# Mixture-of-experts kernel: chunks routed one by one, POOL left with indirect DMAs alone, one region per expert, tiles in two rounds of 24 and 47

## The reference

```python
x = x + relu(conv3x3_8_groups(ln_c(x)) + bias)
t = to_tokens(x)                                   # 4096 tokens of 128
flat = ln_t(t)
logits = flat @ router_w.T                         # 8 experts
topk_vals, topk_idx = top_k(logits, 2)
topk_w = softmax(topk_vals)
y_e = (silu(flat @ w_gate[e]) * (flat @ w_up[e])) @ w_down[e]   # 128 -> 256 -> 128
t = t + sum over a token's two experts of topk_w * y_e
```

## Time and profile before

| | |
|---|---|
| three runs, median (lowest to highest) | 278.57 us (277.93 to 279.11) |
| span of the profiled execution | 277.2 us |
| its own time | not given beside the span; the median lies 1.4 us over the span |
| TensorE busy (matmuls) | 202.9 us, 73% |
| POOL busy | 163.6 us, 59% |
| DVE busy | 140.8 us, 51% |
| ACT busy | 119.0 us, 43% |
| mean granted TensorE clock | 0.866 |

### The profile page before, as it was taken

The page is one execution under the profiler, slowest core; times in us unless marked ns, Lnnn a source line. Parts: engine busy times, 40 slices in busy tenths (PEclk is TensorE's granted clock), DMA queues, the critical chain, the costliest instruction groups (busy, mean ns, idle before and its releaser), DMA issues.

```text
span 277.2 us, 4518 instructions
## 1 busy us (share of the span) xinstructions
PE 202.9 (73%) x1186; PEld 174.3 (63%) x1186; DVE 140.8 (51%) x457; ACT 119.0 (43%) x285; POOL 163.6 (59%) x184
## 2 busy tenths in 40 slices
PE   6699576975529595739998654993999999999000
PEld 5687464864428484428887544883898789898000
DVE  3557696555241724445755322451458866555025
ACT  2369544745902353073453322342445454454100
POOL 5644388743775277725777777764356576666600
PEclk9599895999957777757999999898899999999855
DMA  7993010100133351100232232343239523361075
GB/s 235 380 381 116 0 48 30 53 29 10 48 94 82 78 115 59 48 10 31 74 87 70 68 78 78 100 134 84 61 68 303 159 72 96 99 195 43 15 237 217
DMA packets 26648, 28.99 MB, mean 105 GB/s; under 512 B 4957, under 2 KB 18409, under 8 KB 26624
## 3 DMA queue, kind: packets, MB, share of 16 engines
q1 hardware_dynamic: 21776, 20.03, 25.1%
q0 software_dynamic: 4544, 8.47, 9.1%
q10 hardware_dynamic: 304, 0.20, 0.2%
HBM read 16.93 MB, written 12.67 MB: 107 GB/s over the span
## 4 chain that ended last, share of the span: by engine, by line
PE 28%; POOL 21%; issue 13%; DVE 12%; DMA 11%; SPq 6%; ACT 6%; POOLq 1%; ACTq 0%; DVEq 0%
POOL zs L992 11%; POOL yb L1005 9%; PE ps_gu L349 7%; PE ps_y L439 5%; DMA yb<-y,zt 3%; PE ps_gu L419 3%; PE ps_gu L421 3%; PE ps_gu L420 3%; PE ps_h L429 3%; SPq L303 3%; DMA zt<-zs 3%; ACT zr L547 2%; DMA spare<-yb 2%; PE ps_z L408 2%; DVE bn L637 2%
## 5 line engine op out<-in xcount | busy, mean ns | idle before, releaser
L1005 POOL DMA_INDIRECT yb<-y,zt x78 | 76.3, 978 | 40.0 <-ACT y L583 24.6
L992 POOL DMA_INDIRECT zs<-zr,slot x64 | 63.0, 984 | 38.0 <-issue 18.3
L349 PE MATMUL ps_gu<-pad,ckw 128*128 128x256 f32 x192 | 53.7, 439 | 0.0
L349 PEld LDWEIGHTS ps_gu<-pad,ckw 128*128 128x128 f32 x192 | 41.7, 224 | 7.1
L842 DVE TENSOR_TENSOR hh<-ps_gu,sg 128x512 f32<-128x512 f32 (+1 forms) x40 | 27.1, 678 | 35.7 <-ACT sg L574 35.7
L439 PE MATMUL ps_y<-wall,hT 128*128 x312 | 41.9, 278 | 0.0
L439 PEld LDWEIGHTS ps_y<-wall,hT 128*128 128x128 f32 x312 | 38.7, 195 | 0.1
L574 ACT ACTIVATE sg<-ps_gu 128x512 f32<-128x512 f32 (+1 forms) x40 | 23.5, 586 | 33.3 <-PE ps_gu L421 33.3
L583 ACT ACTIVATE y<-ps_y,zt 128x128 f32<-128x128 f32 x78 | 24.4, 365 | 30.1 <-PE ps_y L439 30.1
L419 PE MATMUL ps_gu<-wall,z_lo 128*128 x78 | 36.4, 467 | 0.0
L408 PE MATMUL ps_z<-ident,zt 128*128 128x128 f32 x78 | 17.1, 302 | 21.2 <-DMA zt<-zs 15.2
(11 more groups left out here) (131 smaller groups left out, 225.9 us busy)
## 6 DMA issues: line engine op xcount, KB each, us to landing
zt<-zs SPq DMA_DIRECT2D x78, 65.0 KB, 2.0
spare<-yb SPq DMA_DIRECT2D x16, 256.0 KB, 4.5
xt<-x_rows SPq DMA_DIRECT2D x8, 256.0 KB, 5.3
xc<-x_cols SPq DMA_DIRECT2D x8, 256.0 KB, 6.6
spare<-gate_up_w SPq DMA_DIRECT2D x8, 256.0 KB, 6.3
out<-xt SPq DMA_DIRECT2D x8, 256.0 KB, 3.0
yb<-y,zt POOLq DMA_INDIRECT x78, 2.3
zs<-nulls SPq DMA_DIRECT2D x18, 65.0 KB, 3.3
```

What stands on the lines that cost most here:

```text
L349: last = nc.tensor.matmul(dst, ckw[:, h * BANDS + k, :], pad[n % 2][:, h * IMG:(h + 1) * IMG, below:below + PAIRS, dx:dx + WW], start=k == ...
L992: nc.gpsimd.indirect_dma_start(zs[g], bass.IndirectOffsetOnAxis(slot[:, k, n * TT + t:n * TT + t + 1], 0), zr[n % ZR][:, t, k, :], None, b ...
L1005: nc.gpsimd.indirect_dma_start(yb, bass.IndirectOffsetOnAxis(zt[:, u % RING, s, P:P + 1].bitcast(U32), 0), y[u % YB][:, s, :], None, bound ...
```

## The change

The order of routing changes from batches of chunks to single chunks, and what POOL does is cut down to constants, three weight tails and indirect DMAs.

- The power -0.5 of both LayerNorms goes from POOL to a square root on ACT (deviation_x, deviation_t) and five small operations on DVE (inverse_x, inverse_t: a reciprocal, one Newton step and the shift).
- rows_and_logits is one product with the identity and the router weights side by side (136 columns); ACT copies the logits and the rows out.
- top_two takes for each tile a max of 8 and a max_index of 8, then two compares with expert numbers. It runs for each chunk in the iteration after its convolution; slots, inverse_t and normalise_t of chunk n-2 run in iteration n. Those of the last chunk's LayerNorm run ahead of unit 0.
- zr has a buffer for each of the 8 chunks, with the token numbers written by POOL at the start. A row has 129 values: the weight no longer travels with it. The weights (gaps, shares, write_shares) are taken once for all tokens in units 3 to 7 and applied by DVE in add_rows, eight operations of 128 columns for a chunk. y_rows becomes one copy.
- POOL scatters all chunks first (dispatch), and only then results.
- There is one region per expert for all tokens. Round 1 has the first 24 full tiles of chunks 0 to 3 (first_table), round 2 the 47 others, sorted by the chunk that completes them (second_table): 12 + 24 = 36 units.
- RING goes from 8 to 18 and the y buffers from 8 to 16 (in the memory of the raw weights).
- SP gathers and stores by chunk: chunks 0 to 3 ahead of unit 30's load, then each later chunk as soon as the last unit that can hold its rows is stored.

The core of the diff:

```diff
-BATCHES = [(0, 1), (1, 2), (2, 4), (4, 6), (6, 8)]
-SETS = [(0, 3), (3, 5)]
-LAST = len(BATCHES) - 1
-SET_OF_BATCH = [g for g, (b0, b1) in enumerate(SETS) for _ in range(b0, b1)]
-BATCH_OF = [b for b, (c0, c1) in enumerate(BATCHES) for _ in range(c0, c1)]
-SET_CHUNKS = [(BATCHES[b0][0], BATCHES[b1 - 1][1]) for b0, b1 in SETS]
-BT = 2 * TT
-NT = [(c1 - c0) * TT for c0, c1 in SET_CHUNKS]
-GOFF = [c0 * N for c0, c1 in SET_CHUNKS]
-CAP = [nt * P + P for nt in NT]
-TILES = [2 * nt + E - 1 for nt in NT]
-SLOTS = [(t + 1) // 2 for t in TILES]
-FIRST = [sum(SLOTS[:g]) for g in range(len(SETS))]
+EARLY = CHUNKS // 2
+CAP = TOK + P
+NULL = E * CAP
+TILES1 = EARLY * N * 2 // P - E
+TILES2 = (CHUNKS - EARLY) * N * 2 // P + 2 * E - 1
+ROUNDS = [TILES1, TILES2]
+SLOTS = [(t + 1) // 2 for t in ROUNDS]
+FIRST = [0, SLOTS[0]]
 UNITS = sum(SLOTS)
-SET_OF_UNIT = [g for g, s in enumerate(SLOTS) for _ in range(s)]
-COUNT = [min(2, TILES[g] - 2 * (u - FIRST[g])) for u, g in enumerate(SET_OF_UNIT)]
-
+ROUND_OF_UNIT = [r for r, s in enumerate(SLOTS) for _ in range(s)]
+COUNT = [min(2, ROUNDS[r] - 2 * (u - FIRST[r])) for u, r in enumerate(ROUND_OF_UNIT)]
+LATE = CHUNKS - EARLY + 1
+NG = LATE * E
+
+
+def last_unit_of(n):
+    tiles = (max(n, EARLY - 1) + 1) * N * 2 // P + E - 1
+    return FIRST[1] + (tiles - TILES1 + 1) // 2 - 1
+
+
+X_GROUPS = [(0, 1), (1, 2), (2, 4), (4, 6), (6, 8)]
+DVE_TAILS = {2: [1, 3], 3: [5, 6], 4: [7]}
 POOL_TAILS = [0, 2, 4]
-DVE_TAILS = [[1, 3], [5, 6], [7]]
-X_GROUPS = [(0, 1), (1, 2), (2, 4), (4, 6), (6, 8)]
-
-ROW = P + 2
+
+ROW = P + 1
 WROW = 2 * 2 * H + 2 * P
-RING = 8
-YB = 8
-ZR = 4
+FUSED = P + E
+RING = 18
+YB = 16
 NOWHERE = 1 << 20
-PIECE = 4
-TABLE_UNIT = 10
+GATHER_AFTER = 30
+TABLE_UNIT = 8
 
 
 def metaformer_moe(nc, x_rows, x_cols, conv_k, conv_b, router, gate_up_w, down_w, out):
...
+            sp.wait_ge(table_ready, 1)
+            for n in range(EARLY):
+                sp.wait_ge(scattered[n], 16 * 2 * TT)
+            for u in range(0, FIRST[1], 4):
+                load_units(u, min(u + 4, FIRST[1]))
+            pad_regions()
+            for n in range(EARLY, CHUNKS):
+                sp.wait_ge(scattered[n], 16 * 2 * TT)
+            sp.wait_ge(nulls_stored, 16 * (E + 1))
+            sp.wait_ge(table_ready, 2)
+            for u in range(FIRST[1], GATHER_AFTER, 4):
+                load_units(u, min(u + 4, GATHER_AFTER))
+            await_results(EARLY - 1)
+            for n in range(EARLY):
+                gather_rows(n)
+            for u in range(GATHER_AFTER, UNITS, 4):
+                load_units(u, min(u + 4, UNITS))
+            await_results(EARLY)
+            gather_rows(EARLY)
+            for n in range(EARLY):
+                store_rows(n)
+            for n in range(EARLY + 1, CHUNKS):
+                await_results(n)
+                gather_rows(n)
+                store_rows(n - 1)
+            store_rows(CHUNKS - 1)
+            sp.wait_ge(out_stored, 16 * CHUNKS)
 
...
             def rows_and_logits(n):
-                b = BATCH_OF[n]
                 pe.wait_ge(t_ready, n + 1)
-                if n >= 2:
-                    pe.wait_ge(t_copied, n - 1)
+                if n >= 1:
+                    pe.wait_ge(t_copied, n)
                 for t in range(TT):
-                    last = nc.tensor.transpose(ps_t[n % 2][:, t * P:(t + 1) * P], xc[:, n, t * P:(t + 1) * P], ident[:])
+                    last = nc.tensor.matmul(ps_t[:, t // 2, t % 2, :], xc[:, n, t * P:(t + 1) * P], ident_x[:],
+                                            start=True, stop=True)
                 last.then_inc(t_rows_ready, 1)
...
+                nc.scalar.copy(logits[:, n * TT:(n + 1) * TT, :].rearrange("p (b t) e -> p b t e", b=2),
+                               ps_t[:, :, :, P:FUSED]).then_inc(logits_ready, 1)
+                nc.scalar.copy(xt[:, n * TT:(n + 1) * TT, :].rearrange("p (b t) c -> p b t c", b=2),
+                               ps_t[:, :, :, 0:P]).then_inc(t_copied, 1)
+
+            def deviation_t(n):
+                i = slice(n * TT, (n + 1) * TT)
+                act.wait_ge(mv2_ready, n + 1)
+                nc.scalar.activation(sd2[:, i], mv2[:, i, 1], ACT.Sqrt, bias=eps[:, 1:2]).then_inc(sd2_ready, 1)
 
             def normalise_t(n):
-                b = BATCH_OF[n]
-                act.wait_ge(rstd2_ready, b + 1)
+                act.wait_ge(rstd2_ready, n + 1)
                 act.wait_ge(t_copied, n + 1)
-                if n >= ZR:
-                    act.wait_ge(scattered[n - ZR], 16 * 2 * TT)
                 for t in range(TT):
                     i = n * TT + t
-                    last = nc.scalar.activation(zr[n % ZR][:, t, :, 0:P], xt[:, i:i + 1, :].broadcast_to([P, 2, P]),
-                                                ACT.Identity, bias=nmr2[:, i:i + 1], scale=rstd2[:, i:i + 1])
-                last.then_inc(z_ready, 1)
...
+            deviation_x(0)
             normalise_x(0)
+            deviation_x(1)
             act.wait_ge(pads_zeroed, 2)
             pad_evens(0)
...
+            for n in range(1, CHUNKS + 1):
+                conv_relu(n - 1, 1)
+                if n == 1:
+                    normalise_x(2)
+                if n in (2, 4):
+                    deviation_x(n // 2 + 2)
+                if n >= 3:
+                    deviation_t(n - 2)
+                    normalise_t(n - 2)
                 if n < CHUNKS:
                     conv_relu(n, 0)
+                copy_rows(n - 1)
                 if n + 1 < CHUNKS:
                     pad_evens(n + 1)
-                if n >= 1:
-                    copy_rows(n - 1)
-                if n < 2:
-                    for e in range(4 * n, 4 * n + 4):
-                        weight_heads(e)
-                for b, (c0, c1) in enumerate(BATCHES[:-1]):
-                    if n == c1:
-                        pair_weight(b)
-                        normalise_t(c0)
-                    if n == c1 + 1 and c1 == c0 + 2:
-                        normalise_t(c0 + 1)
+                if n == 1:
+                    deviation_t(0)
+                    normalise_t(0)
+                if n + 2 < CHUNKS:
+                    normalise_x(n + 2)
+                if 2 <= n <= 6:
+                    weight_heads((1, 3, 5, 6, 7)[n - 2])
+            deviation_t(CHUNKS - 1)
+            normalise_t(CHUNKS - 1)
             z_heads(0)
             for u in range(UNITS + 2):
                 if u + 1 < UNITS:
                     z_heads(u + 1)
                 if u < UNITS:
                     silu(u)
-                if u == 0:
-                    pair_weight(LAST)
-                if u <= 1:
-                    normalise_t(CHUNKS - 2 + u)
+                if u == 4:
+                    shares()
...
-                    last = nc.scalar.activation(y[u % YB][:, s, :], ps_y[u % 2][:, s * P:(s + 1) * P], ACT.Identity,
-                                                scale=zt[:, u % RING, s, P + 1:P + 2])
-                last.then_inc(y_ready, 1)
...
+            def inverse_t(n):
+                i = slice(n * TT, (n + 1) * TT)
+                dve.wait_ge(sd2_ready, n + 1)
+                nc.vector.reciprocal(guess2[:, i], sd2[:, i]).then_inc(dev2_step, 1)
+                dve.wait_ge(dev2_step, 4 * n + 1)
+                nc.vector.scalar_tensor_tensor(off2[:, i], mv2[:, i, 1], EPS_FFN, guess2[:, i], ALU.add, ALU.mult
+                                               ).then_inc(dev2_step, 1)
+                dve.wait_ge(dev2_step, 4 * n + 2)
+                nc.vector.scalar_tensor_tensor(half2[:, i], off2[:, i], -0.5, guess2[:, i], ALU.mult, ALU.mult
+                                               ).then_inc(dev2_step, 1)
+                dve.wait_ge(dev2_step, 4 * n + 3)
+                nc.vector.scalar_tensor_tensor(rstd2[:, i], half2[:, i], 1.5, guess2[:, i], ALU.add, ALU.mult
+                                               ).then_inc(dev2_step, 1)
+                dve.wait_ge(dev2_step, 4 * n + 4)
                 nc.vector.scalar_tensor_tensor(nmr2[:, i], mv2[:, i, 0], -1.0, rstd2[:, i], ALU.mult, ALU.mult
                                                ).then_inc(rstd2_ready, 1)
 
...
+            def top_two(n):
+                dve.wait_ge(logits_ready, n + 1)
+                for t in range(TT):
+                    last = nc.vector.max(top8[:, n * TT + t, :], logits[:, n * TT + t, :])
+                last.then_inc(top_ready, 1)
+                dve.wait_ge(top_ready, n + 1)
+                for t in range(TT):
+                    last = nc.vector.max_index(which8[:, t, :], top8[:, n * TT + t, :],
+                                               logits[:, n * TT + t, :])
+                last.then_inc(which_ready, 1)
+                dve.wait_ge(which_ready, n + 1)
+                for k in range(2):
+                    last = nc.vector.tensor_tensor(oh[:, k], ioe[:, k],
```

(65 more changed lines are left out.)

790 lines of the change are left out of this document (334 added, 456 removed).

## The result

The changed kernel takes 247.87 us (median of four runs, 246.16 to 248.83), the kernel before 278.25 us beside it (four runs, 277.71 to 279.11): a ratio of 0.891, 95% interval 0.887 to 0.896. Ratios here leave out executions more than 1.5% above the fastest of the same kernel; medians take all. The forecast was 245. The profiled execution has a span of 245.9 us and a time of its own of 248.08.

The account below looks back on a forecast made before the run. TensorE was held by 23 us of gaps from late scatters and a ring of 8, then by 2.94 us units. 109.7 + 5 + 35 x 2.94 = 217.6; + 9.3 + 16.8 = 243.7; + 1.4 = 245.1, range 234 to 258.

Parts of the forecast that it names:

- a ring of 8 and POOL's alternating scatters: Between routing and full expert work: tile loads wait for combines and late scatters; the 23 us of TensorE gaps go.
- POOL was to catch up at unit 12: Combines start at 128, 2.55 us a unit against results 2.94 apart, so POOL catches up at unit 12.
- Tiles: Expert stage: 36 units instead of 40, 4 x 2.94 = 11.8 us less, exact while TensorE is the limit.
- Routing: Routing stage: a DVE and ACT loop of 10.5 us sets the chunks; first gate-up at 109.7, no gain at its end.
- R1: First residual in routing, forecast at 21.2 us, against 22.14 before.
- R2 to R3: Second to third residual in routing, forecast as 7.9 us, putting R3 at 41.5.
- The searches: top_two in the routing loop: eight searches at 0.16 us each plus 0.6, 1.9 us per chunk.
- The rival of two passes: Index search in routing loads its values first: 5 to 7 us more, 250 to 252; chance 0.23.
- The table load: Silu's table load on ACT in round 1: 1.28 us by the trace, 2.66 by the skill, giving 245 or 246.5.
- Half clock in routing: Rival: TensorE at half clock through routing, 13.6 us a chunk instead of 10.5, +19, 264; chance 0.09.
- Round 1: First 12 units, 109.7 to about 150: 5 us added to the pace (3 to 10) for second table and slow first unit.
- The tail: After last gate-up: 9.3 us to the end of sum 3, sums 1.8 each, then 16.8 of gather, sum, store turns.

Follow-up runs that it names:

- kernel 4: The kernel before, with all of the last two chunks scattered by POOL before its first combine, rings still 8 units: 278.0 us beside 277.4, ratio 1.002.
- kernel 5: The kernel before, with rings of 16 units for tiles and results in place of 8: 271.0 us, ratio 0.980.
- kernel 6: The kernel before, with both rings of 16 units and all scatters ahead of the first combine: 270.3 us, ratio 0.977.
- kernel 12: The kernel before, with rings of 16, all scatters first, and the first set's gather and sums 4 and 8 units later: 263.4 us, ratio 0.949.
- kernels 1 and 8: Kernel 1: the changed kernel, with the last two chunks' scatters put between the combines of units 0 to 7, 263.4 us; for the other see kernel 8.
- kernel 7: The changed kernel, with every max and max_index of the routing stage done a second time into unread buffers: 252.8 us.
- kernel 10: The changed kernel, with VectorE's second table split over units 2, 3 and 4 instead of all in unit 2: 244.3 us.
- kernel 8: The changed kernel, with SP's gathers of chunks 5, 6 and 7 no longer behind the stores of chunks 3 to 6: 240.7 us, ratio 0.867.

## Why the prediction was right, and where not

**What bounds the kernel, and what would go.** Right: a ring of 8 and POOL's alternating scatters made the gaps, and 23.8 us of gaps and of slow units behind them went. But the prediction names these two and the table as what holds the tiles up, and the kernel before held more. There the order alone is worth 0 (kernel 4), the rings 7.2 (kernel 5), both 8 (kernel 6), and 6.9 more come only with the later gather and sums (kernel 12). The profiles, from the first residual to the end, say the same: 255.1 before, then 257.6, 247.5, 246.7 and 240.4. In the changed kernel taking the order back costs 15.5, the rings 9.0. Each is a gate in front of the same tiles, so a gain shows only when the last one opens. The prediction didn't see that the place of the gather was such a gate; the change moves it too, so the sum came out, in that part by luck. Behind it stands POOL's own pace (kernel 12). With that the prediction had reckoned: POOL was to catch up at unit 12, and it did at unit 7's combine (145.67).

**Tiles.** 11.8 forecast, "exact", for four units of 2.94. It is 10.6, since one of the four had one tile (the books above). Seven tiles put back cost 12.6, 9.6 of it for the tiles between the gate-ups, the rest a stall of their own and the tail. The pace per unit is right, the count of four full units is not; no term of the sum rests on it, which goes by 35 x 2.94.

**Routing.** Forecast: residuals from 21.2 to 98.3, first gate-up 109.7. Measured: 23.36 to 98.48, and 109.80. The end agrees, some terms not: R1 came 2.2 late, since the first convolution half ran at the lower clock; R2 to R3 took 8.9 instead of 7.9; the loops with the table and behind it took 12.2, 11.3 and 8.8 instead of 12.9, 10.7 and 9.8. From R3 to R5 it took 21.7 (10.97 and 10.71) instead of 23.4, so that most of the 1.3 and 1.1 us added for stats_x and inverse_x doesn't show. The errors, +2.2, +1.0, -1.7 and (behind R5) -1.2, cancelled: that the end agrees to 0.2 us is luck. (R1 is the first residual, as in the prediction.)

**The searches.** The rows of VectorE:

```profile
26.44 0.37 DVE L729 MAX8 top<-logits 128x8 f32<-128x8 f32 x4 [2.38 <-ACT logits L550]
26.84 0.09 DVE L733 MATCH_VALUE_LOAD which<-top,logits 128x8 f32 x1
26.92 0.16 DVE L733 FIND_INDEX8 which<-top,logits 128x8 uint32<-128x8 f32 x1
27.00 0.07 DVE L733 MATCH_VALUE_LOAD which<-top,logits 128x8 f32 x1
27.06 0.16 DVE L733 FIND_INDEX8 which<-top,logits 128x8 uint32<-128x8 f32 x1
```

The rival of two passes named what happens, and not its price. A search for positions is two instructions, but from one pair to the next it is 0.13 to 0.16 us, and the four MAX8 take 0.37: top_two is over in 1.6 us, 1.9 forecast. The Trainium skill (Vector Engine (DVE) Microarchitecture Reference, 3.9 The match/index hardware and the swap-based sort pattern) gives the search as MATCH_VALUE_LOAD and then FIND_INDEX_8, and the rows agree. The 5 to 7 us that I had hung on it came from pricing the load as a whole small operation.

**The table load.** One behind the start, at 110.57, of 1.28 us, with ScalarE waiting for TensorE behind it. The rows, with those of the load at the start:

```profile
2.32 1.28 ACT L606 ACT_TABLE_LOAD   x1 [2.32 <-issue]
3.62 0.20 ACT L606 ACTIVATE th<-eps 128x2 f32<-128x2 f32 x1
...
110.18 0.37 ACT L582 CAST z_hi<-ps_z 128x256 fp32r<-128x256 f32 x1 [1.30 <-PE ps_z L417]
110.57 1.28 ACT L590 ACT_TABLE_LOAD   x1
112.74 0.60 ACT L590 ACTIVATE sg<-ps_gu 128x512 f32<-128x512 f32 x1 [0.89 <-PE ps_gu L430]
```

The Trainium skill (ScalarE: Activation LUTs, What ACT_TABLE_LOAD costs) puts a drain of 1380 ns beside a switch, 2.66 us in all. These rows have no room for it. The load at 110.57 begins 0.02 us behind the cast, silu begins 2.19 us behind the cast in all, and the last 0.89 of that are put down to TensorE. Behind the load at the start the next operation begins after 0.02 us. The measurement decides: 1.28 us, the price that the sum went by. That no load stands between Sqrt and Relu, copy or Identity agrees with what the prediction took from the same page.

**Half clock in routing.** The rival gave 264. The mean clock did fall (0.80, not the 0.85 of the earlier trace rows), and it cost about 4 us, all at the start: kernels 1 and 8, at full clock there, had R1 at 20.6 and 20.4 (23.4 here) and R3 7.7 behind R2 (8.9 here, at a granted clock of 0.62). 7.9 was forecast. From R3 on their distances are those of the changed kernel to 0.1 us: VectorE's list is the limit there, as kernel 7 shows.

**Round 1.** 5 us over the pace forecast, 5.3 measured (108.51 less 35 x 2.95). Most of it is the second table, 4.4 us in one piece on VectorE (118.53 to 122.94): the split (kernel 10) gives 3.0 back. Last gate-up 217.6 forecast, 218.31 measured.

**The tail.** This is the term that was mis-sized: a sum of 1.8 us, priced as small operations of 32 columns, is 2.3, with 348 ns for one operation of 128 columns and 0.28 from one to the next. The end of sum 3 is thereby at 229.4 instead of 226.9 (11.1 us behind the last gate-up, 9.3 forecast). From there the 16.8 forecast were 16.5, by the very turns described, and kernel 8 shows that these turns, not the DMAs or the last combine, set it. So the 2.9 us between 245 and 247.9 are 0.7 up to the last gate-up, 1.8 for the sums, -0.3 for the turns and 0.8 around the span (2.2 instead of 1.4).

## What to carry to other kernels

When several waits stand before the same work, opening one can give nothing: before a gain is put down to one edit, find the wait that ends next, and look also in the lists of engines that are not named (here VectorE, held by a sum whose gather waited for POOL, and behind that POOL's own pace). A queue that alternates gathers and stores in order ties each load to the sum before it; issue what can go first. Work that is moved into a pipeline's loop should be cut in pieces as small as the engine's free time in a unit.
